# Third attention of a four-layer block: centred key and query weights, biases as matrix products, another order of the queues

## Chip, core and metric
One NeuronCore of a Trainium2 chip runs one program. The metric is the device time of one execution in microseconds; three executions were timed, and one more was profiled.

## What is computed
Four layers, each an attention-like part and a feed-forward network (FFN), add to one residual x of 1024 rows (4 batches of 256) by 256 columns. The change concerns the third attention:

```python
q = _ln((x @ Wq + bq).reshape(b, s1, H, HD), qn_w, qn_b)         # H = 16 heads, HD = 16
k_dca = _ln((y[:, -16:] @ Wkv_dca + bkv_dca)[keys], kn_dca_w, kn_dca_b)   # last 16 context rows
k = _ln(y[:, :-16] @ Wk + bk, kn_w, kn_b)                        # the other 240
ctx = softmax(q k / 4) v + softmax(q k_dca / 4) v_dca            # two softmaxes, added
x = x + ctx @ Wo + bo
```
The layer norm `_ln` works per head over 16 columns. (These lines are condensed.)

## The kernel before
Five in-order queues (TensorE, VectorE, ScalarE, GpSimd, SyncE for transfers) are written out by hand; counting semaphores tie them. Rows lie on 128 partitions in 8 tiles; `X` holds the residual. PSUM has 8 banks of 512 f32 columns. Work of neighbouring layers is interleaved by hand:
- **482.8 to 540** (times of the profile): the second FFN for its first 512 rows. TensorE's `gate_up(0, 0, c)` (L2338) makes chunk c of 8, ScalarE's `silu` and VectorE's `gate` (L1632) finish it. Between the chunks stand tiles 4 to 7 of the first, quantised FFN: `ffn0_gate_up`, `ffn0_gated` (L1428: two products, block maxima), GpSimd's scaling, `ffn0_round`, scaling, `hidden_transpose`, `ffn0_down`. `gate_up` chunk 6 asks for the first product of tile 7.
- **540 to 557**: the second attention's last batches, the norms, the four down products.
- **557 to 628.7**: the second FFN for the other 512 rows, 8 chunks and 4 down products, with the third attention's keys between. `K_STEPS` (L394) says which key steps stand after which chunk. A key batch is 256 context rows: `keys_values` (L2265) makes three products of 512 columns (keys and values of two tiles, and the 16 extra rows' own weights applied to the second tile). VectorE's `keys_step` (L1574) adds biases, masks, centres (`center`, L1507), squares and sums (`variance`), divides by the root (`over_deviation`), applies gains, and merges the third product's keys into the second tile. ScalarE takes the root (L954, with a table of its own, so that each use loads two tables).
- Keys and queries are split into three bf16 parts each, six slots of 16 columns a head (`kparts`): ScalarE's copies, and two subtractions on VectorE (L1614, L1595; L1744, L1746 for queries). TensorE transposes this stack in four quarters of four heads (`stack_transpose`, L2253), all through banks 0 and 1, and ScalarE copies each quarter out (`stack_out`, L981).
- `queries(hf, part)` (L1531) does the like for 512 query rows (four tiles, 1024 columns a pass): the first half between the down products, the second in batch 0's loop.
- **628.7 to 670.5**: query stacks of batches 0 and 1, then `scores` (L2479) for 16 heads of batch 0, each read by two maximum reductions (L1753 over 240 keys, L1754 over 16) from one of two banks, then `maxima_parts` (L1756).
- **670.5 to 820**: the loop over 4 batches of 16 heads. Each head has a transposed score with the maximum subtracted (`shifted`, L2497), `Exp`, and `values` (L2510). Beside them stand the next batch's scores and maxima, its query stack, the second queries (batch 0), `normalise` (L1766) every four heads, output products, and steps of a table lookup for the third FFN's weights (`lut_step`, L1785, with ScalarE's L1082). GpSimd makes `shiftw` (L661) before it.

## Time and profile before
| what | us |
|---|---|
| median of 3 runs (lowest, highest) | 1001.25 (999.36, 1004.71) |
| the profiled execution | 998.12 |
| its span | 996.30 |
| TensorE busy | 869.7 |
| VectorE busy | 681.3 |
| ScalarE busy | 547.3 |
| GpSimd busy | 360.5 |

The span runs from the first to the last instruction recorded; times in the views count from its start. Matrix products are pipelined, and their ends are modelled. An f32 product shows as two instructions. Engines are PE (TensorE), PEld (its weight loads), DVE (VectorE), ACT (ScalarE), POOL (GpSimd).

### The profile page before, as it was taken

To read this page: it belongs to the slowest core of one execution; us is meant where nothing else is said; L and a number is where in the kernel's file an instruction comes from. 1 tells how busy PE (TensorE), PEld (TensorE's weight loads), DVE (VectorE), ACT (ScalarE), POOL (GpSimd) and SP (SyncE) were. 2 spreads that over 40 slices of the span, in tenths; PEclk is the share of its full clock that TensorE was granted. 3 is DMA by queue.
4 is the path that set the end of the run, shared out by engine and by line. 5 is a ranking of instruction groups with operands and counts; after the bars stand their busy time and mean duration, and the time that the engine had idled before them with its cause. 6 is when DMAs were issued, how large, how long until landed. Compare 5 with 4: busy or idle time off the path is not lost.

```text
span 996.3 us, 13312 instructions
## 1 busy us (share of the span) xinstructions
PE 869.7 (87%) x4446; PEld 612.8 (62%) x4450; DVE 681.3 (68%) x1369; ACT 547.3 (55%) x1017; POOL 360.5 (36%) x249
## 2 busy tenths in 40 slices
PE   4797799999999999987888889458789899999998
PEld 3365587777778778744446546327578784554646
DVE  4347689899998988786765766666888872453211
ACT  2377577877877777974333444435678672012110
POOL 1211578787877778656443100030000000700000
PEclk9899899999999999999999999759699999999999
DMA  4003000001000000110302000000000002000000
GB/s 130 17 0 143 16 17 16 16 16 32 16 16 16 16 19 4 46 43 1 112 10 86 0 1 1 0 1 1 1 2 1 2 1 104 32 1 1 16 5 22
DMA packets 12926, 24.27 MB, mean 24 GB/s; under 512 B 4281, under 2 KB 8657, under 8 KB 11729
## 3 DMA queue, kind: packets, MB, share of 16 engines
q1 hardware_dynamic: 12448, 20.53, 6.5%
q10 hardware_dynamic: 432, 3.15, 0.8%
q8 instruction: 27, 0.44, 0.2%
q14 instruction: 19, 0.15, 0.0%
HBM read 22.63 MB, written 1.05 MB: 24 GB/s over the span
## 4 chain that ended last, share of the span: by engine, by line
PE 34%; DVE 15%; ACT 5%; issue 3%; POOL 2%; DMA 0%; ACTq 0%; DVEq 0%; POOLq 0%
PE PS L2344 14%; PE PS L2356 6%; PE PS L2522 3%; DVE mxf L1753 2%; PE PS L2131 1%; PE PS L2261 1%; PE PS L1865 1%; POOL regA L620 1%; ACT regC L1082 1%; PE PS L2204 1%; PE PS L2296 1%; PE PS L2486 1%; PE PS L2506 1%; PE PS L2507 1%; ACT regA L1097 1%
## 5 line engine op out<-in xcount | busy, mean ns | idle before, releaser
L541 POOL TENSOR_TENSOR X<-X,xn 128x512 f32<-128x512 f32 x62 | 103.4, 1668 | 69.0 <-ACT xn L771 68.3
L500 POOL TENSOR_SCALAR veps<-mv 128x4 f32<-128x4 f32 (+1 forms) x20 | 5.5, 275 | 299.9 <-DVE mv L1154 297.9
L1238 DVE TENSOR_SCALAR_CACHE_REDUCE regA<-PS,nrq 128x256 bf16<-128x256 f32 x128 | 56.0, 475 | 37.9 <-PE PS L1940 36.0
L1261 DVE TENSOR_TENSOR_SCAN regB<-regB 128x1024 f32<-128x1024 f32 x30 | 78.5, 2618 | 1.1 <-POOL regA L620 1.0
L534 POOL TENSOR_TENSOR y<-y,regB 128x1024 f32<-128x1024 f32 x32 | 75.6, 2365 | 9.4 <-DVE regB L1272 9.3
L795 ACT ACTIVATE regA<-PS,nb,rq 128x256 f32<-128x256 f32 x128 | 72.1, 576 | 11.7 <-DVE regA L1238 10.9
L2522 PE MATMUL PS<-regA 128*128 128x128 f32 x512 | 73.3, 289 | 3.4 <-ACT regA L1097 3.1
L1962 PE MATMUL PS<-regA 128*128 128x256 f32 x256 | 67.0, 384 | 7.3 <-DVE qss L1225 7.2
L2522 PEld LDWEIGHTS PS<-regA 128*128 128x128 f32 x512 | 66.5, 202 | 7.3 <-ACT regA L1097 6.2
L1940 PE MATMUL PS<-regA 128*128 128x256 f32 x256 | 67.8, 388 | 0.0
L1971 PE MATMUL PS<-regA 128*128 128x256 f32 x256 | 66.3, 382 | 0.0
L1913 PE MATMUL PS<-xnT,regA 128*128 128x512 f32 x128 | 60.6, 616 | 4.6 <-ACT regA L761 3.4
L2344 PE MATMUL PS<-xnT,regB 128*128 128x512 f32 x128 | 59.3, 609 | 1.4 <-DMA regB<-in_wd 1.4
L2356 PE MATMUL PS<-regB 128*128 128x256 f32 x256 | 57.0, 379 | 0.0
L2344 PE MATMUL PS<-regA,regB 128*128 128x512 f32 x128 | 55.8, 594 | 1.4 <-ACT regA L1010 1.4
L1962 PEld LDWEIGHTS PS<-regA 128*128 128x128 f32 x256 | 47.3, 192 | 14.2 <-DVE qss L1225 8.4
L1940 PEld LDWEIGHTS PS<-regA 128*128 128x128 f32 x256 | 46.4, 194 | 15.5 <-issue 10.1
L1002 ACT ACTIVATE regB<-PS 128x512 f32<-128x512 f32 (+1 forms) x28 | 16.7, 595 | 69.6 <-PE PS L2344 63.2
L801 ACT COPY regA<-PS 128x512 f32<-128x512 f32 x64 | 38.2, 596 | 29.8 <-PE PS L1951 29.6
L1640 DVE TENSOR_TENSOR regB<-regB,PS 128x512 f32<-128x512 f32 (+1 forms) x28 | 19.2, 686 | 50.9 <-ACT regB L1002 50.9
L1971 PEld LDWEIGHTS PS<-regA 128*128 128x128 f32 x256 | 49.2, 192 | 6.9
L771 ACT ACTIVATE xn<-PS,ls 128x256 f32<-128x256 f32 x124 | 52.8, 491 | 0.1
(285 smaller groups left out, 2103.8 us busy)
## 6 DMA issues: line engine op xcount, KB each, us to landing
regA<-in_W SPq DMA_DIRECT2D x16, 384.0 KB, 3.0
regB<-in_wg SPq DMA_DIRECT2D x2, 1024.0 KB, 6.3
regB<-in_wu SPq DMA_DIRECT2D x2, 1024.0 KB, 8.2
X<-in_x SPq DMA_DIRECT2D x1, 1024.0 KB, 8.1
regC<-in_wg ACTq DMA_DIRECT2D x1, 1024.0 KB, 5.9
regC<-in_wu ACTq DMA_DIRECT2D x1, 1024.0 KB, 8.0
regC<-in_wd ACTq DMA_DIRECT2D x1, 1024.0 KB, 11.1
regB<-in_wd SPq DMA_DIRECT2D x1, 1024.0 KB, 4.8
```

The source lines that it names most:

```text
L534: pool.tensor_tensor(halves(y3, i), halves(y3, i), halves(prod, i), ALU.add).then_inc(y_done, 1)
L541: pool.tensor_tensor(xt, xt, part, ALU.add).then_inc(x0_add, 1)
L795: act.activation(p0[i][:, q, :], bank(S_BANK + i)[:, q * S:(q + 1) * S], ACT.Exp, bias=nb0[:, i, q:q + 1], scale=rq[par][:, 2 * b + q:2 * ...
L1238: ins = dve.tensor_scalar(spill[:, i, q, :], bank(S_BANK + i)[:, q * S:(q + 1) * S], nrq[par][:, t:t + 1], None, ALU.mult, ALU.min, accum_ ...
L1261: dve.tensor_tensor_scan(v(hs), v(decays), v(dBu), 0.0, ALU.mult, ALU.add).then_inc(scan_done, 1)
L1913: last = pe.matmul(to[:, i * HALF:(i + 1) * HALF], w0[par][:, c * P:(c + 1) * P], xnT[:, c, i * HALF:(i + 1) * HALF], start=c == 0, stop=c ...
L1940: last = pe.matmul(bank(S_BANK + b % 2)[:, q * S:(q + 1) * S], qT[par][:, (2 * b + q) * P:(2 * b + q + 1) * P], kT[par][:, b * S:(b + 1) * S],
L1962: last = pe.matmul(bank(O_BANK)[:, 0:S], ctxN[:, 2 * b + k, :], pT0[b % 2][:, k, :], start=k == 0, stop=k == 1)
L1971: last = pe.matmul(bank(W_BANK)[:, q * DIM:(q + 1) * DIM], oT0[b % 2][:, q * P:(q + 1) * P], wvo[par], start=True, stop=True)
L2344: last = pe.matmul(bank(to)[0:rows, :], w[:, k, c * P:c * P + rows], src[:, k, :], start=k == 0, stop=k == KD - 1)
L2356: last = pe.matmul(bank(6 + td % 2)[:, 0:DIM], hT[0:rows, c, t * P:(t + 1) * P], wd[0:rows, c, :], start=c == 0, stop=c == nch - 1)
L2522: last = pe.matmul(bank(6 + g % 2)[:, at:at + P], pT2[i % 3][:, k, q * P:(q + 1) * P], V2flat[:, v:v + P], start=k == 0, stop=k == 1)
```

## The change
1. VectorE subtracts each head's mean over its 16 columns from the key and query weights and biases (`center_weights`, four steps between pieces of the first FFN), so that projections come out centred. The biases become three bf16 parts, and TensorE adds them by a product with a 0/1 matrix, `pick`.
2. A key batch takes two tiles in place of three. GpSimd copies the 16 extra context rows into `ctx_extra` (zeros elsewhere) and zeroes them in `ctxT`, so that their product adds into the second tile's bank. Gains come laid out per row (`gain_k`).
3. ScalarE squares out of PSUM and copies and masks the values; VectorE sums squares, divides out of PSUM and applies gains. ScalarE's root takes scale and offset.
4. Stack quarters 1 and 3 are copied out by VectorE (until the first query stack), 0 and 2 by ScalarE.
5. The first queries move among the chunks (after chunk 3), and the order of all queues around them is rewritten. The scores of batch 0 use four banks and stand between the down products.
6. A maximum is one reduction into groups of 16 keys, joined once a batch. `normalise` does one product in place of two; GpSimd adds the output bias. Steps in the loop move by a head (`STACK2`, `LNT9`, `QPROJ`, `QNORM`). Some buffers share memory in another way.

The core of the diff (eight leading blanks dropped):

```diff
+bc3 = max_groups[0:96].rearrange("p h q g -> p (h q g)").bitcast(BF16)
...
+KV_BANK = [4, 6, 6, 6]
+NORM2 = ["k0", "k1", "k2", "q0", "k3", "q1"]
...
+def by_vector(k):
+    return k < 4 * (B + 1) and k % 2
+def copied(k):
+    if by_vector(k):
+        return stk_copy, sum(1 for i in range(k + 1) if by_vector(i))
+    return stk_out, sum(1 for i in range(k + 1) if not by_vector(i))
+def score_bank(b, h):
+    return 2 + (h % 4 if b == 0 else h % 2)
...
+    for tile, name in ((wkv2, "wkv2"), (wdca2, "wdca2"), (wq2, "wq2"), (bias_rows, "b2"), (pick_rows, "pick"), (wo2, "wo2")):
         sp.dma_start(tile, a[name]).then_inc(ld_2, 16)
-    for tile, name, n in ((bkv2[:, 0:DIM], "bk2", DIM), (bkv2[:, DIM:], "bv2", DIM), (bdca2, "bdca2", 2 * DIM),
-                          (bq2, "bq2", DIM), (bo2, "bo2", DIM)):
-        sp.dma_start(tile, a[name].to_broadcast([P, n])).then_inc(ld_2, 16)
...
+    last_keys = ctxT[:, :].rearrange("p (b two k) -> p b two k", b=B, two=2)[:, :, 1, MAIN - P:]
+    pool.wait_ge(y_done, 2 * NST + 1)
+    pool.wait_ge(qk1_mm, 2)
+    pool.memset(ctx_extra[:, :, 0:MAIN - P], 0.0).then_inc(ctx_set, 1)
+    pool.tensor_copy(ctx_extra[:, :, MAIN - P:], last_keys).then_inc(ctx_set, 1)
+    pool.wait_ge(ctx_set, 2)
...
+    def output_bias(hf):
+        pool.wait_ge(*xn_ready(8 + hf))
+        for i in range(2):
+            xt = X[:, TPH * hf + 2 * i:TPH * hf + 2 * i + 2, :]
+            pool.tensor_tensor(xt, xt, bo2.unsqueeze(1).to_broadcast([P, 2, DIM]), ALU.add).then_inc(bo2_add, 1)
...
+    def squares(name):
+        dst = qs[int(name[1])] if name[0] == "q" else k_sq
+        if name[0] == "q":
+            act.wait_ge(q2_mm, int(name[1]) + 1)
+        else:
+            act.wait_ge(kv2_mm, int(name[1]) + 1)
+        if name in ("k1", "k2", "k3"):
+            act.wait_ge(var2, norm2("k%d" % (int(name[1]) - 1)))
+        act.activation(dst.rearrange("p t h d -> p t (h d)") if name[0] == "k" else dst.rearrange("p (a t) h d -> p a (t h d)", a=2),
+                       qk_bank(name).rearrange("p a h d -> p a (h d)"), ACT.Square).then_inc(sq2, 1)
+    def values_out(b):
+        act.wait_ge(kv2_mm, b + 1)
+        v = [bank(KV_BANK[b] + t)[:, DIM:].rearrange("p (h d) -> p h d", h=H2) for t in range(2)]
+        act.copy(V2[:, 2 * b, :, 0:HD2], v[0])
+        act.activation(V2[:, 2 * b + 1, :, 0:HD2], v[1], ACT.Copy, scale=mask[:, 0:1])
+        act.activation(V2[:, 2 * b + 1, :, HD2 + 1:VW - 1], v[1], ACT.Copy, scale=mask[:, 1:2]).then_inc(v2_out, 1)
+    def deviations(name):
+        lo, n = (4, TPH) if name[0] == "q" else (0, 2)
+        act.wait_ge(var2, norm2(name))
+        act.activation(r2[:, lo:lo + n, :], m2[:, lo:lo + n, :], ACT.Sqrt, scale=1.0 / HD2, bias=qk_eps[:, 0:1]).then_inc(dev2, 1)
...
+    silu(0, 1, 0)
+    squares("k1")
+    values_out(1)
+    silu(0, 1, 1)
+    stack_even(0)
+    ln_apply(8)
+    deviations("k1")
+    silu(0, 1, 2)
     ln_out(8)
...
+    keys_high(1)
+    keys_mid(1)
+    silu(0, 1, 3)
+    squares("k2")
+    squares("q0")
+    values_out(2)
+    silu(0, 1, 4)
+    deviations("k2")
+    deviations("q0")
+    stack_even(1)
+    silu(0, 1, 5)
+    keys_high(2)
+    squares("k3")
+    keys_mid(2)
+    values_out(3)
+    silu(0, 1, 6)
+    deviations("k3")
+    stack_even(2)
+    keys_high(3)
+    silu(0, 1, 7)
+    keys_mid(3)
+    stack_high(0)
+    stack_even(3)
+    stack_mid(0)
+    stack_even(B)
...
+    def center_weights(step):
+        dve.wait_ge(ld_2, LD2)
+        if step == 0:
+            both = regC[:, 0:4 * DIM].rearrange("p (w s h d) -> p w s h d", w=2, s=2, h=H2)[:, :, 0]
+            center(both, m2[:, 8:10, :]).then_inc(w2_ready, 1)
+        elif step == 1:
+            center(groups(wq2.rearrange("p k n -> p (k n)")), m2[:, 10:12, :].rearrange("p a h -> p (a h)")).then_inc(w2_ready, 1)
+        elif step == 2:
+            dve.tensor_copy(pick.rearrange("p a m -> p (a m)"), pick_rows).then_inc(w2_ready, 1)
+            link(center(groups(bias_rows[:, 0:2 * DIM]), m2[0:96, 6:8, :].rearrange("p a h -> p (a h)")))
+        else:
+            link(dve.tensor_copy(bias3, bias_rows))
+            link(dve.tensor_tensor(bias_rows, bias_rows, bias3, ALU.subtract))
+            dve.tensor_copy(bias3[32:64], bias_rows[32:64])
+            link(dve.tensor_copy(bias3[64:96], bias_rows[64:96]))
+            link(dve.tensor_tensor(bias_rows[64:96], bias_rows[64:96], bias3[64:96], ALU.subtract))
+            dve.tensor_copy(bias3[64:96], bias_rows[64:96]).then_inc(w2_ready, 1)
+    def variances(name):
+        lo, n, v = (4, TPH, qs[int(name[1])]) if name[0] == "q" else (0, 2, k_sq)
+        dve.wait_ge(sq2, norm2(name))
+        dve.tensor_reduce(m2[:, lo:lo + n, :], v, AX.X, ALU.add).then_inc(var2, 1)
+    def normed(name):
+        b = int(name[1])
+        lo, n, v = (4, TPH, qf[b % 2]) if name[0] == "q" else (0, 2, kf)
+        r, flat_r = r2[:, lo:lo + n, :], r2[:, lo:lo + n, :].rearrange("p t h -> p (t h)")
+        dve.wait_ge(dev2, norm2(name))
+        link(dve.reciprocal(r, r))
+        if name[0] == "q":
+            src = qk_bank(name)
+            by = flat_r.rearrange("p (a g) -> p a g", a=2).unsqueeze(3).to_broadcast([P, 2, 2 * H2, HD2])
+            link(dve.tensor_tensor(v.rearrange("p (a t) h d -> p a (t h) d", a=2), src, by, ALU.mult))
+            dve.sem_inc(q2_out, 1)
+            wide = [P, TPH * H2, HD2]
+            link(dve.tensor_tensor(rows_of(v), rows_of(v), ln2[:, 0, :].unsqueeze(1).to_broadcast(wide), ALU.mult))
+            dve.tensor_tensor(rows_of(v), rows_of(v), ln2[:, 1, :].unsqueeze(1).to_broadcast(wide), ALU.add).then_inc(stk_f, 1)
+        else:
+            wide = [P, 2, H2, HD2]
+            link(dve.tensor_tensor(v, qk_bank(name), r.unsqueeze(3).to_broadcast(wide), ALU.mult))
+            dve.sem_inc(kv2_use, 1)
+            link(dve.tensor_tensor(v, v, gain_k[:, 0].unsqueeze(2).to_broadcast(wide), ALU.mult))
+            dve.tensor_tensor(v, v, gain_k[:, 1].unsqueeze(2).to_broadcast(wide), ALU.add).then_inc(stk_f, 1)
+    def keys_rest(b):
+        dve.wait_ge(stk_h, b + 1)
+        dve.tensor_tensor(ks2, kf2, kparts[:, :, 0, :], ALU.subtract).then_inc(stk_r, 1)
+    def keys_low(b):
+        dve.wait_ge(stk_m, b + 1)
+        dve.tensor_tensor(kparts[:, :, 2, :], ks2, kparts[:, :, 1, :], ALU.subtract).then_inc(stk_done, 1)
+    def stack_odd(j):
+        for c in (1, 3):
+            b = j % B
+            dve.wait_ge(stk_tr, 4 * j + c + 1)
+            src = bank(1).bitcast(BF16)[0:STK, :].rearrange("p (h t) -> p h t", h=HPB)
+            heads = slice(HPB * c, HPB * c + HPB)
+            dve.tensor_copy(ksT[:, heads, b * S:(b + 1) * S] if j < B else qsT[b % 2][:, heads, :], src).then_inc(stk_copy, 1)
...
     gate(0, 0, 2)
     ffn0_round(4)
     gate(0, 0, 3)
+    center_weights(0)
     ffn0_gated(5)
     gate(0, 0, 4)
     ffn0_round(5)
+    center_weights(1)
     ffn0_add(4)
     ffn0_gated(6)
     gate(0, 0, 5)
     ffn0_round(6)
+    center_weights(2)
     ffn0_add(5)
+    center_weights(3)
     ffn0_gated(7)
...
+    gate(0, 1, 0)
+    variances("k1")
+    stack_odd(0)
+    gate(0, 1, 1)
+    normed("k1")
+    keys_rest(1)
+    gate(0, 1, 2)
+    keys_low(1)
+    gate(0, 1, 3)
+    variances("k2")
+    variances("q0")
+    gate(0, 1, 4)
+    normed("k2")
+    normed("q0")
+    stack_odd(1)
+    keys_rest(2)
+    gate(0, 1, 5)
+    variances("k3")
+    keys_low(2)
+    gate(0, 1, 6)
+    normed("k3")
+    stack_odd(2)
+    keys_rest(3)
+    gate(0, 1, 7)
+    keys_low(3)
     ffn_add(0, 1, 0)
...
+    stack_rest(0)
+    stack_odd(3)
+    stack_low(0)
+    stack_odd(B)
...
-        sc = bank(2 + h % 2).rearrange("p (q k) -> p q k", q=2)
         dve.wait_ge(s2_mm, i + 1)
-        dve.tensor_reduce(mxf[:, :, h, 0], sc[:, :, 0:MAIN], AX.X, ALU.max)
-        dve.tensor_reduce(mxf[:, :, h, 1], sc[:, :, MAIN:], AX.X, ALU.max).then_inc(max2, 1)
+        dve.tensor_reduce(max_groups[:, h], bank(score_bank(b, h)).rearrange("p (q g k) -> p q g k", q=2, k=DCA), AX.X,
+                          ALU.max).then_inc(max2, 1)
...
+        dve.tensor_reduce(mxf[:, :, :, 0].rearrange("p q h -> p h q"), max_groups[:, :, :, 0:MAIN // DCA], AX.X, ALU.max)
+        link(dve.tensor_copy(mxf[:, :, :, 1].rearrange("p q h -> p h q"), max_groups[:, :, :, MAIN // DCA]))
...
+        link(dve.reciprocal(rl2[:, :, :].rearrange("p n s -> p (n s)"), o[:, :, HD2]))
+        link(dve.tensor_tensor(co2.rearrange("p n s d -> p (n s) d"), o[:, :, 0:HD2],
+                               rl2[:, :, :].rearrange("p n s -> p (n s)").unsqueeze(2).to_broadcast([P, 4 * HPB, HD2]), ALU.mult))
+        parts = co2.rearrange("p (h q) s d -> p q h s d", q=2)
+        dve.tensor_tensor(co[:, :, HPB * g:HPB * g + HPB, :], parts[:, :, :, 0, :], parts[:, :, :, 1, :], ALU.add).then_inc(o2_norm, 1)
...
+        if b == 0:
+            pe.wait_ge(w2_ready, 4)
+            pe.wait_ge(ctx_set, 3)
+            pe.wait_ge(gated, FC)
+        elif b == 1:
+            pe.wait_ge(df_add, TPH)
         else:
...
+            pe.wait_ge(kv2_use, b)
+            pe.wait_ge(v2_out, b)
+        for t in range(2):
+            to, td = bank(KV_BANK[b] + t), 2 * b + t
+            pe.matmul(to, ctxT[:, td * P:(td + 1) * P], wkv2, start=True, stop=False)
+            if t:
+                pe.matmul(to, ctx_extra[:, b, :], wdca2, start=False, stop=False)
+            last = pe.matmul(to, pick[:, t, :], bias3[:, DIM:], start=False, stop=True)
+        last.then_inc(kv2_mm, 1)
...
+                    pe.matmul(to, xnT[:, k, td * P:(td + 1) * P], wq2[:, k, :], start=k == 0, stop=False)
+                last = pe.matmul(to, pick[:, 0, :], bias3[:, 0:DIM], start=False, stop=True)
+        last.then_inc(q2_mm, 1)
...
-    ln_transpose(8)
+        if c == 0:
+            keys_values(1)
+        elif c == 1:
+            stack_keys(0)
+        elif c == 2:
+            pe.wait_ge(*copied(2))
+            pe.wait_ge(*copied(3))
+            ln_transpose(8)
+        elif c == 3:
+            keys_values(2)
+            queries(0)
+        elif c == 4:
+            pe.wait_ge(q2_out, 1)
+            stack_keys(1)
+        elif c == 5:
+            keys_values(3)
+        elif c == 6:
+            stack_keys(2)
+    pe.wait_ge(kv2_use, B)
+    pe.wait_ge(v2_out, B)
     pe.wait_ge(df_add, TPH)
...
+        pe.wait_ge(*copied(4 * (B + b) + h // HPB))
+        if b == 0 and h < 4:
+            pe.wait_ge(gated, 2 * FC)
+        elif b == 0:
+            pe.wait_ge(max2, h - 3)
+        elif h >= 2:
             pe.wait_ge(max2, i - 1)
+        else:
+            pe.wait_ge(max2, b * H2)
         for q in range(2):
-            last = pe.matmul(bank(2 + h % 2)[:, q * S:(q + 1) * S], qsT[b % 2][:, h, q * P:(q + 1) * P],
+            last = pe.matmul(bank(score_bank(b, h))[:, q * S:(q + 1) * S], qsT[b % 2][:, h, q * P:(q + 1) * P],
...
+        if h % HPB == HPB - 1 and h < H2 - 1:
+            pe.wait_ge(df_add, TPH + h // HPB)
+            down(0, 1, h // HPB + 1, wf_d)
```

## Rows read from the trace of the kernel before
**Rows 1.** The page, parts 1 and 2: busy time, and granted clock by slice.
```profile
PE 869.7 (87%) x4446; PEld 612.8 (62%) x4450; DVE 681.3 (68%) x1369; ACT 547.3 (55%) x1017; POOL 360.5 (36%) x249
...
PEclk9899899999999999999999999759699999999999
```

**Rows 2.** Windows: stretch in us; its length; busy us (instructions) per engine; clock; DMA share, GB/s.
```profile
482.82:540.00 57.18, 48.49 (x196) 23.66 (x196) 35.70 (x60) 18.83 (x30) 24.97 (x21) 1.00 0.26 78
...
557.00:608.50 51.50, 42.74 (x148) 21.17 (x147) 39.57 (x89) 28.50 (x36) 1.86 (x4) 0.93 0.00 0
608.50:628.70 20.20, 20.16 (x120) 17.71 (x120) 13.70 (x23) 6.44 (x8) 0.00 (x0) 1.00 0.00 1
628.70:670.50 41.80, 16.64 (x99) 9.18 (x99) 25.11 (x57) 15.86 (x18) 7.02 (x1) 0.61 0.00 1
670.50:718.00 47.50, 37.08 (x255) 32.04 (x255) 34.96 (x82) 26.42 (x36) 1.27 (x2) 0.77 0.00 1
718.00:753.00 35.00, 28.41 (x249) 24.89 (x249) 29.34 (x73) 27.58 (x42) 0.00 (x0) 1.00 0.00 1
```

**Rows 3.** Timeline, TensorE: start us, us, engine, line, operation, count, [idle before <- releaser].
```profile
624.20 1.06 PE L2261 MATMUL PS<-identb,regB 128*96 128x128 bf16 x16
...
637.95 1.94 PE L2261 MATMUL PS<-identb,regB 128*96 128x128 bf16 x16 [9.18 <-DVE regB L1595]
...
647.24 1.91 PE L2261 MATMUL PS<-identb,regB 128*96 128x128 bf16 x16 [5.42 <-DVE regB L1746]
...
657.21 1.25 PE L2486 MATMUL PS<-regA,regB 96*128 96x256 bf16 x4 [5.22 <-DVE mxf L1754]
```

**Rows 4.** Groups by shape, 557 to 670.5, VectorE: busy us, mean ns | idle before.
```profile
L1753 DVE TENSOR_REDUCE mxf<-PS 128x2 f32<-128x480 f32 x16 | 10.5, 656 | 0.7
...
L1520 DVE TENSOR_TENSOR regB<-regB,r 128x768 f32<-128x768 f32 x4 | 3.8, 958 | 0.1
...
L1754 DVE TENSOR_REDUCE mxf<-PS 128x2 f32<-128x32 f32 x16 | 2.9, 182 | 0.0
...
L1606 DVE TENSOR_TENSOR regB<-regB,ln 128x512 f32<-128x512 f32 x4 | 2.8, 692 | 0.1
...
L1519 DVE RECIPROCAL r<-r 128x48 f32<-128x48 f32 x3 | 1.4, 453 | 1.7 <-ACT r L954 1.7
L1550 DVE TENSOR_TENSOR regB<-regB,ln 128x1024 f32<-128x1024 f32 x1 | 1.2, 1226 | 0.0
```

**Rows 5.** The same view, 0 to 480, VectorE: its casts to bf16.
```profile
L1186 DVE CAST bc<-PS 96x512 bf16<-96x512 f32 x2 | 1.4, 686 | 2.1 <-PE PS L1880 2.0
...
L1188 DVE CAST bc<-regC 32x512 bf16<-32x512 f32 x2 | 0.8, 416 | 0.1
```

**Rows 6.** Timeline, VectorE and TensorE, around 523.
```profile
522.13 1.48 DVE L1435 TENSOR_TENSOR regA<-regA,PS 128x512 f32<-128x512 f32 x2 [0.18 <-ACT regA L910]
...
524.25 3.65 PE L2344 MATMUL PS<-xnT,regB 128*128 128x512 f32 x8
```

**Rows 7.** Groups by shape, 557 to 670.5, ScalarE.
```profile
L987 ACT COPY regA<-PS 96x1024 bf16<-96x1024 bf16 x16 | 15.3, 1007 | 20.9 <-PE PS L2261 20.9
L1002 ACT ACTIVATE regB<-PS 128x512 f32<-128x512 f32 x8 | 4.8, 594 | 6.2 <-PE PS L2344 6.2
...
L1072 ACT COPY regB<-PS 96x256 bf16<-96x256 bf16 x1 | 0.4, 368 | 14.3 <-PE PS L2493 14.3
```

**Rows 8.** Timeline, TensorE: two chunks of gate and up products.
```profile
571.63 4.34 PE L2344 MATMUL PS<-xnT,regB 128*128 128x512 f32 x8
...
576.70 3.65 PE L2344 MATMUL PS<-xnT,regB 128*128 128x512 f32 x8
```

**Rows 9.** Timeline, ScalarE: a table load and the instruction behind it.
```profile
562.26 1.28 ACT L1002 ACT_TABLE_LOAD   x1
563.55 0.60 ACT L1002 ACTIVATE regB<-PS 128x512 f32<-128x512 f32 x1
```

**Rows 10.** Timeline, TensorE: a wait for maxima in batch 0's loop.
```profile
696.59 0.58 PE L2486 MATMUL PS<-regA,regB 96*128 96x256 bf16 x2 [3.64 <-DVE mxf L1754]
```

417 lines of the change are left out of this document (166 added, 251 removed).

## The prediction
> **What bounds the kernel now.** I read the page first: TensorE is busy 87% of the span at a clock granted 8 tenths or more nearly everywhere, except in two slices, 7 and 5 [rows 1]. A stretch where TensorE idles and is slow is where a rescheduling can pay. The table of stretches places it [rows 2]. Six stretches matter: 482.8 to 540 (the first half of the second FFN interleaved with the quantised one), 557 to 608.5 (second half, gate and up products, with the key batches between), 608.5 to 628.7 (down products, first queries), 628.7 to 670.5 (query stacks, scores, maxima of batch 0), 670.5 to 718 (loop over the heads of batch 0), and a later batch. In the fourth TensorE works 16.6 of 41.8 us at a clock of 0.61; batch 0's loop takes 47.5 us where the next takes 35. From 557 to 670.5 VectorE is busy 39.6 + 13.7 + 25.1 = 78.4 of 113.5 us. The timeline shows TensorE waiting for VectorE's norms and splits: gaps of 9.2, 5.4 and 5.2 us [rows 3]. The same work hangs from one queue in batch 0's loop, where VectorE is busy 35.0 us.
>
> **The centring of weights, 482.8 to 540.** New: VectorE centres the key and query weights and builds three-part bf16 biases in four steps, between pieces of the FFN. Steps 0 and 1 are a reduce, a small scale and a subtract over 512 columns: 0.7 + 0.2 + 0.7 = 1.6 us each, by the 512-column row [rows 4]. Step 2 is a small cast and the same on 96 partitions, 1.8. Step 3 is four casts of 768 columns (0.55 each, from 0.42 for 512 [rows 5]) and two subtracts of 0.96 [rows 4], 4.1. Sum 9.1 us. VectorE idles 57.2 - 35.7 = 21.5 us here [rows 2], but the places are bad. Step 0 stands right behind a gate and ahead of the quantised FFN's tile 5, step 1 ahead of tile 6; each hands on most of its 1.6 us. Steps 2 and 3 (5.9 us) stand ahead of its last tile, now at 522.13 after a wait of 0.18 [rows 6]. TensorE's chunk 6 waits for the first half of that tile and starts at 524.25, some 1.4 us after it. Tile 7 comes 1.7 (the delay handed on from steps 0 and 1) + 5.9 late, chunk 6 is 7.6 - 1.4 = 6.2 late, and the last hidden block, behind it, as much. I take **+7 us**, with 0.3 for the three bias products, plus 1 for the gap's clock: **+8**. Bounds: 1 (all falls into idle time) and 11 (the 9.1 whole, and 2 of clock). The new waits ahead of the first key product (weights, context, gate 7) end with or before that tile; behind them stand attention 1 and the down products, all shifted by the same 8. SP issues 11 transfers in place of 13 on that semaphore, before its wait for the quantised FFN's last product, as now; the index loads behind move with the 8 and have 100 us. GpSimd's zeroing and copying of context columns, some 1 us, falls into idle time.
>
> **One key batch.** VectorE now spends eight instructions on copying, biasing and masking out of PSUM, five 768-column passes (0.96 each), six on gains and masks, two of 0.69 on splits: 13 us. After: a reduce of 512, a reciprocal of some 0.4, three passes of 512 (0.69 [rows 4]), two splits, 4.6 us, plus two of the four stack copies that ScalarE has at 1.0 us each [rows 7]. No row copies bf16 from PSUM on VectorE. The nearest is 96x512 of f32 at 0.69 [rows 5], so for 1024 columns twice that less the overlap; bounds 0.8 (twice the SBUF cast's 0.42) and 1.37. I take 1.15, the nearest: 6.9 us in all. The Trainium skill ("VectorE: DVE Perf Modes", the perf-mode tier table) lets a copy that touches PSUM reach up to 2x when all is 16-bit; by it a copy would take 0.6 and the stretch would end 1.4 us earlier. ScalarE gains a square (0.6) and three value copies (0.4 each) [rows 7].
>
> **The queries.** Ten passes (two of 512, eight of 1024 columns) with smalls, 10.8 us per half, become a reduce, a reciprocal of 0.55 and three passes of 1.23 [rows 4]: 5.5 us.
>
> **The stretch 557 to 670.5, as one schedule.** I laid the four queues out in order with these durations, 0.15 us from a signal to its waiter, and TensorE at the upper clock: 3.5 us a chunk [rows 8], 3.0 for a key product (6 x 0.43, two bf16 bias products of 0.22), 3.9 for the queries, 0.45 per stack quarter (16 transposes take 1.06 with overlap [rows 3]), 0.22 per head of scores. TensorE's sum is 68. The stops:
> 1. Each set of four transposes waits for copies: 0.8 us, five times.
> 2. After chunk 4 comes a wait of 6.7 us: it asks for the first queries' read-out from PSUM, which on VectorE stands behind key batch 2, which waits for ScalarE's square roots, which stand behind silu of that very chunk. Then 1.4 more for the copy behind the query gains.
> 3. Chunk 6's stack waits 2.4 + 2.3 for the roots and copies of batch 3, the query stack 2.3 for its low part.
> 4. The last four heads' maxima and the five small steps behind (1.75) leave 4.0 and 0.7 idle before the first shifted score.
> These make 23.9, and the first shifted score comes 92 us after the start, against 113.5: **-21.5**. Gate and up alone end at 61.5, later than 51.5 now, since the queries are among them; scores and maxima hide between down products, which cover 12 of the 16. A chunk behind a wait took 4.34 us at a lower clock, for 3.65 [rows 8]; two such losses after stop 2: **+1.5**. Bounds for the stretch: -30 (stop 2 gone) and -12 (the clock low for half of it).
> The root tables: 1.28 us a load; eight here, as the schedule has them. In the trace the silu starts 0.01 us after its load's end [rows 9]. The Trainium skill ("ScalarE: Activation LUTs", what ACT_TABLE_LOAD costs) adds a drain of 1.38 us to each; the row speaks against it, and by it my schedule would end 2.8 us later.
>
> **The loop, 670.5 to 820.** Batch 0: TensorE waits for VectorE, up to 3.64 us, while the second queries' passes stand ahead of the maxima [rows 10], so 10.8 - 5.5 = 5.3 us of query work come off; with one block of queries in place of three, some 2 more of low clock (0.77 [rows 2]): -7. A maximum is one pass of 512, at 0.62, for 0.66 + 0.18 overlapped to 0.67 [rows 4]; the joining of groups costs 0.85 a batch: 16 x 0.05 - 0.85, nothing. Normalisation and the output bias, moved to idle GpSimd (4 additions), take 0.3 us off each batch. Together **-8**; bounds 0 and -12. Behind 820 nothing changes.
>
> **Sum:** +8 - 21.5 + 1.5 - 8 = -20. The profiled execution took 998.12 (span 996.30), 3.1 under the median of 1001.25; I set the difference against the median: **981 us**.
>
> **The rivals.**
> *The centring is covered and the loop runs freer.* For it: 21.5 idle us of VectorE, so a delay can be absorbed. Then +2 instead of +8 and -11 instead of -8: 972. Against: the two late steps come in one block before a tile that two chunks ask for.
> *In-order queues tie up.* Three engines now hand each key batch around inside one chunk; any estimate 0.3 us short is paid at each hand-over, about 30 of them: +9, 990. For it: stops 2 and 3 are of this kind already. Against: each link above is priced from a row.
> *Slower: TensorE stays at 1.2 GHz from stop 2 on.* The place is the 6.7 us gap after chunk 4. The schedule behind it holds 36 us of TensorE work and 15 of waiting: at the lower clock +36 - 15 = +21. Batch 0's loop has 37.1 x 0.77 = 28.6 us of work, 57 at the lower level against my 40: +17. Together 981 + 38 = 1019. It decides from the point where the clock is still low when the loop begins: by then 21 us have gone, of 20 gained, and every further head costs. For it: 0.61 over 41.8 us now, with gaps of this size. Against: a chunk at a lower clock took 4.34 us and the next 3.65 [rows 8], so chunks bring the clock back, and three follow. The Trainium skill ("TensorE: Matmul & The Clock Gate", HAM oscillation) warns of just such gaps between bursts; the rows agree that the clock falls, and that it returns.
> *No gain:* stretch at its bound -12, centring at 11, loop 0: 1000.
>
> **How the numbers follow.** A difference of 0.5% is about what a measurement of this kernel can tell from none. Forecast 0.60 (its own range 973 to 989), freer 0.15, tied up 0.16, no gain 0.05, slow clock 0.04. No gain and slow clock (0.09) lie outside the range, and a third of the two rivals beside the forecast (0.10): 966 to 994. Faster by over 0.5%: 0.60 + 0.15 + 0.16 = 0.91, and 0.01 of the fourth; same 0.04, slower 0.04.
>
> **What would show it.** (a) TensorE idle for some 5 us ahead of chunk 6 of the first half, ended by VectorE. (b) From that half's last down product to the first shifted score about 92 us. (c) A TensorE gap of 5 to 8 us after the fifth chunk, ended by VectorE. (d) Batch 0's loop about 40 us, the next 34 to 35. (e) VectorE's stack copies at 1.15. (f) Clock over 0.85 in the stretch now at 0.61. It is wrong if (b) exceeds 105, if chunk 6 does not wait, or if the loop keeps its 47 us.

## The result, and the profile after
The kernel after takes **991.98 us** (median of 6, 989.88 to 994.31), the kernel before, beside it, 1001.24 (median of 6): a ratio of 0.9906 with a 95% interval of 0.9882 to 0.9929. It is faster, by 9.3 us, where 20 were forecast: 0.9%, and the interval leaves out 1. The profiled execution took 989.88 us, with a span of 988.1. So the two profiles differ by 8.2 us of span. The page of the kernel after answers to [rows 1]:

```profile
PE 871.6 (88%) x4462; PEld 615.1 (62%) x4466; DVE 653.4 (66%) x1237; ACT 546.9 (55%) x1026; POOL 366.3 (37%) x257
...
PEclk8899799999999999999997998889899999899999
```
VectorE has 28 us less work, and the slices at 7 and 5 of [rows 1] are gone, and the one at 6 two slices later. But the clock now dips (the 7 in slice 22, 519 to 543 us) where the second FFN's first half stands. Five marks split the span in both profiles: the first chunk of the second FFN's first half, that of its second half, the first shifted score, the transposes of batch 1's maxima, and the third FFN's first chunk (stretches 1 to 5 start there).

| stretch | before | after | difference | forecast |
|---|---|---|---|---|
| ahead of 1 | 487.7 | 488.3 | +0.7 | 0 |
| 1: first half, with the quantised tiles | 69.6 | 81.3 | +11.7 | +8 |
| 2: second half, to the first shifted score | 113.3 | 96.0 | -17.2 | -20 |
| 3: batch 0's loop, to batch 1's maxima | 47.4 | 42.8 | -4.6 | -7 |
| 4: the other batches | 104.5 | 102.8 | -1.7 | -1 |
| 5: third FFN and all behind | 173.9 | 176.8 | +2.9 | 0 |

The windows of the kernel after, as in [rows 2] (the last two lines are stretches 1 and 2 as a whole):

```profile
483.00:540.00 57.00, 42.90 (x149) 19.33 (x150) 40.48 (x60) 14.45 (x22) 21.70 (x16) 0.88 0.15 48
570.00:622.00 52.00, 44.10 (x183) 24.04 (x182) 25.20 (x48) 29.04 (x45) 4.35 (x6) 0.93 0.00 0
622.00:634.50 12.50, 8.58 (x38) 5.15 (x36) 5.28 (x9) 7.37 (x10) 0.00 (x0) 0.73 0.01 1
634.50:665.70 31.20, 22.88 (x160) 19.08 (x158) 21.54 (x38) 9.05 (x10) 7.02 (x1) 0.90 0.00 1
665.70:708.50 42.80, 34.17 (x257) 29.34 (x258) 30.75 (x63) 28.47 (x39) 4.11 (x4) 0.88 0.00 1
720.00:754.00 34.00, 28.90 (x253) 25.52 (x252) 29.48 (x60) 26.19 (x41) 0.00 (x0) 1.00 0.00 1
488.33:569.66 81.33, 68.24 (x270) 39.72 (x273) 47.66 (x86) 25.91 (x42) 27.44 (x32) 0.92 0.14 47
569.66:665.70 96.04, 75.91 (x376) 48.46 (x374) 52.02 (x94) 45.80 (x63) 11.37 (x7) 0.90 0.00 1
```
Before, stretch 1 ran at a granted clock of 1.00, now at 0.92. The loss there is gaps and clock together. The timeline of TensorE in stretch 1, after:

```profile
508.98 3.70 PE L2488 MATMUL PS<-xnT,regB 128*128 128x512 f32 x8 [0.65 <-DVE regA L1551]
...
519.03 5.40 PE L2488 MATMUL PS<-xnT,regB 128*128 128x512 f32 x8 [1.59 <-DVE regA L1551]
...
534.59 6.25 PE L2488 MATMUL PS<-xnT,regB 128*128 128x512 f32 x8 [5.40 <-DVE regA L1551]
```
Three chunks wait for the quantised tiles, 7.6 us in all. Two of them then take 5.40 and 6.25 us in place of 3.65 [rows 8], 4.3 us more at the lower clock. VectorE's and GpSimd's timelines show one step ahead of those waits:

```profile
514.55 0.68 DVE L1626 TENSOR_REDUCE m<-regC 128x32 f32<-128x512 f32 x1
515.26 1.46 DVE L1627 TENSOR_SCALAR m<-m 128x32 f32<-128x32 f32 x1
516.76 0.69 DVE L1628 TENSOR_TENSOR regC<-regC,m 128x512 f32<-128x512 f32 x1
```
```profile
514.78 1.91 POOL L662 TENSOR_TENSOR regA<-regA,mx_s 128x1024 bf16<-128x1024 fp8e4 x1 [1.20 <-DVE regA L1523]
```
The scale of 32 columns, 0.18 us elsewhere, ends when GpSimd's instruction does (514.78 + 1.91 = 516.69). In step 2 it takes 1.26 in the same way, so 2.4 us of VectorE's queue are such holds (below, "held" means this: an instruction on VectorE that lasts until GpSimd's ends). The Trainium skill ("SBUF — State Buffer", section "Who interferes with whom") describes this: VectorE and GpSimd share a pair of ports, and a fast copy or scale, or an instruction with two SBUF inputs, blocks until the other engine's instruction is through (in the last case only if GpSimd's reads SBUF). The trace agrees: the two scales end with GpSimd's instruction.

In stretch 2 the stops stand where they were forecast ("stack 2" below is the set of transposes of key batch 2, and so on):

```profile
607.38 1.94 PE L2405 MATMUL PS<-identb,regB 128*96 128x128 bf16 x16 [6.78 <-DVEq L1666]
...
624.88 0.88 PE L2405 MATMUL PS<-identb,regB 128*96 128x128 bf16 x8 [2.41 <-ACT regA L1057]
...
627.26 1.06 PE L2405 MATMUL PS<-identb,regB 128*96 128x128 bf16 x8 [1.50 <-DVE regA L1694]
...
642.13 1.94 PE L2405 MATMUL PS<-identb,regB 128*96 128x128 bf16 x16 [2.32 <-DVE regB L1854]
...
664.73 0.42 PE L2646 MATMUL PS<-identb,mxs 128*96 128x128 bf16 x2 [3.89 <-DVE mxs L1904]
```
Sixteen transposes behind a stop take 1.94 us, elsewhere 1.06. TensorE is idle for 20.1 us of the 96.0 in all (34.0 of 113.3 before). One hold was not foreseen: the lookup table's subtract, beside GpSimd's product for `shiftw` (VectorE, then GpSimd):

```profile
646.66 2.60 DVE L1921 TENSOR_TENSOR lutd<-lut 128x8 f32<-128x8 f32 x1
```
```profile
642.22 7.02 POOL L719 TENSOR_TENSOR regC<-regC 96x4096 bf16<-96x4096 f32 x1 [54.56 <-DVE regB L1854]
```

### The profile page after: what moved, and what is told of

Its sections match the earlier page's. It is cut to its first block, busy times and chain, and to the rows that moved or that the text cites. A ratio compares the mean times of both kernels' runs of the same rounds, so it can differ in the third digit from the quotient of the medians.

```text
span 988.1 us, 13238 instructions
## 1 busy us (share of the span) xinstructions
PE 871.6 (88%) x4462; PEld 615.1 (62%) x4466; DVE 653.4 (66%) x1237; ACT 546.9 (55%) x1026; POOL 366.3 (37%) x257
## 4 chain that ended last, share of the span: by engine, by line
PE 39%; DVE 11%; ACT 4%; issue 3%; POOL 1%; DMA 0%; ACTq 0%; DVEq 0%
PE PS L2488 16%; PE PS L2500 7%; PE PS L2675 3%; DVE max_groups L1891 2%; PE PS L2405 1%; PE PS L2275 1%; PE PS L2009 1%; PE PS L2348 1%; PE PS L2659 1%; PE PS L2440 1%; PE PS L2422 1%; PE PS L2660 1%; ACT regB L1077 1%; ACT regC L1197 1%; DVE regB L1937 1%
## 5 line engine op out<-in xcount | busy, mean ns | idle before, releaser
L583 POOL TENSOR_TENSOR X<-X,xn 128x512 f32<-128x512 f32 x62 | 103.5, 1669 | 68.8 <-ACT xn L829 68.0
L853 ACT ACTIVATE regA<-PS,nb,rq 128x256 f32<-128x256 f32 x128 | 72.0, 575 | 11.7 <-DVE regA L1354 10.9
L2675 PE MATMUL PS<-regA 128*128 128x128 f32 x512 | 71.3, 284 | 4.0 <-ACT regA L1210 3.9
L2488 PE MATMUL PS<-xnT,regB 128*128 128x512 f32 x128 | 64.3, 650 | 8.9 <-DVE regA L1551 7.6
L2500 PEld LDWEIGHTS PS<-regB 128*128 128x128 f32 x256 | 48.1, 190 | 7.6 <-issue 1.4
```

Source lines behind the costliest of these rows:

```text
L583: pool.tensor_tensor(xt, xt, part, ALU.add).then_inc(x0_add, 1)
L853: act.activation(p0[i][:, q, :], bank(S_BANK + i)[:, q * S:(q + 1) * S], ACT.Exp, bias=nb0[:, i, q:q + 1], scale=rq[par][:, 2 * b + q:2 * ...
L2488: last = pe.matmul(bank(to)[0:rows, :], w[:, k, c * P:c * P + rows], src[:, k, :], start=k == 0, stop=k == KD - 1)
L2500: last = pe.matmul(bank(6 + td % 2)[:, 0:DIM], hT[0:rows, c, t * P:(t + 1) * P], wd[0:rows, c, :], start=c == 0, stop=c == nch - 1)
L2675: last = pe.matmul(bank(6 + g % 2)[:, at:at + P], pT2[i % 3][:, k, q * P:(q + 1) * P], V2flat[:, v:v + P], start=k == 0, stop=k == 1)
```

## The experiments
Each kernel is the kernel after with one edit, unless said otherwise; "stretch 1" and so on come from its one profile. How far does a stretch repeat where nothing in it was edited? With the kernel after counted in, stretch 1 took 81.3 to 81.6 us (9 profiles) and stretch 2 took 95.6 to 97.5 (7; 96.0 to 96.2 in the 3 whose stretch 1 was unedited too). Stretch 3 took 42.6 to 44.5 (13), stretch 4 102.8 to 106.2 and stretch 5 173.5 to 176.8 (all 15). Effects under these spreads can't be read from one profile, and the intervals of most single edits' totals overlap with that of the kernel after (0.9882 to 0.9929).

| kernel | median us | ratio to before, 95% | 1 | 2 | 3 | 4 | 5 |
|---|---|---|---|---|---|---|---|
| before_again | 1000.63 | 1.0012 (0.9993 to 1.0032) | 69.6 | 113.6 | 47.5 | 104.5 | 175.4 |
| no_centre | 983.03 | 0.9819 (0.9787 to 0.9852) | 71.3 | 95.9 | 44.5 | 105.0 | 175.2 |
| c_moved | 989.80 | 0.9893 (0.9859 to 0.9927) | 78.4 | 95.6 | 44.4 | 105.0 | 175.2 |
| c_moved_stt | 986.61 | 0.9849 (0.9808 to 0.9891) | 73.0 | 97.5 | 43.0 | 103.5 | 175.2 |
| centre_spread | 982.26 | 0.9815 (0.9775 to 0.9855) | 69.9 | 96.7 | 42.9 | 102.9 | 176.8 |
| q0_first | 988.82 | 0.9885 (0.9852 to 0.9919) | 81.4 | 95.4 | 43.1 | 103.5 | 175.2 |
| roots_early | 987.71 | 0.9883 (0.9866 to 0.9899) | 81.3 | 92.2 | 42.9 | 103.5 | 175.2 |
| stacks_first | 990.27 | 0.9908 (0.9879 to 0.9937) | 81.4 | 94.0 | 43.8 | 104.1 | 175.1 |
| copies_scalar | 989.68 | 0.9902 (0.9883 to 0.9922) | 81.5 | 94.5 | 43.6 | 106.2 | 173.6 |
| scores_after | 992.69 | 0.9928 (0.9902 to 0.9954) | 81.3 | 99.6 | 42.6 | 102.9 | 175.2 |
| lutd_early | 990.68 | 0.9899 (0.9858 to 0.9940) | 81.4 | 95.1 | 43.2 | 106.2 | 173.6 |
| split_q1 | 993.66 | 0.9922 (0.9896 to 0.9948) | 81.6 | 96.2 | 43.8 | 105.5 | 175.2 |
| no_q1_gains | 990.28 | 0.9904 (0.9871 to 0.9937) | 81.4 | 96.1 | 40.5 | 105.4 | 175.2 |
| joined | 976.73 | 0.9755 (0.9729 to 0.9781) | 69.9 | 88.3 | 43.7 | 106.2 | 173.5 |
| joined_scalar | 975.33 | 0.9748 (0.9720 to 0.9775) | 71.6 | 93.3 | 44.0 | 104.2 | 175.2 |

**What the centring costs (no_centre).**
```diff
 if step == 2:
     dve.tensor_copy(pick..., pick_rows).then_inc(w2_ready, 1)
-    link(center(groups(bias_rows[:, 0:2 * DIM]), ...))
-else: (casts and subtracts of three parts)
+elif step == 3:
+    dve.tensor_copy(bias3, bias_rows).then_inc(w2_ready, 3)
```


> Leaves out the centring of the key and query weights and of the biases, and the second and third bf16 parts of the biases: VectorE keeps one small cast and one cast of 768 columns of about 9 us of steps. Theory (the missing gain is the centring, whose places delay chunks 4 to 6 of the quantised second FFN half and cost clock behind each gap): the stretch from the first chunk of the second FFN's first half to the first chunk of its second half, 69.6 us before and 81.3 us after the change, comes to 71 +- 1.5, TensorE no longer waits over 1 us ahead of chunks 5 and 6, nothing else moves by over 2 us, and the total is 982 +- 2. Rival (the hand-over of the third attention's first key batch or the longer FFN order makes it, and the centring only fills idle time): the stretch stays over 78 and the total over 988.

Left out are the centring and two of the three parts of the biases. Stretch 1 fell to 71.3, the total by 9 us. The theory stands: some 10 of the 11.7 us are the centring's own. The one large cast left was held as well: it took 2.02 us for 0.55, and chunk 6 waited 0.31 us and took 5.40.

**The same steps elsewhere (c_moved, and c_moved_stt).**
```diff
 ffn0_round(4)
-gate(0, 0, 3)
 center_weights(0)
+gate(0, 0, 3)
 ffn0_gated(5)
+center_weights(1)
...
 ffn0_gated(7)
 layer_norm_stats(6, 0)
+center_weights(3)
...
 ffn0_add(6)
+center_weights(4)
```


> The whole change, with the same centring steps at other places of VectorE's order: step 0 ahead of gate 3 in place of behind it, steps 1 and 2 behind the quantised FFN's tiles 5 and 6 in place of ahead of tiles 6 and 7, step 3 cut in two, both halves behind tile 7. Theory (the price is the place: what stands ahead of a tile delays a chunk): the stretch of 81.3 us comes to 74 +- 2, chunk 6's wait of 5.4 us to under 1.5, total 985 +- 2. Rival (VectorE lacks the time, wherever the 9 us stand): the waits only move to chunks 7 and the first down product, the stretch stays over 79, total 990 or more.

78.4: neither as forecast nor unchanged. The wait ahead of chunk 6 went. The waits inside the quantised tiles stayed or grew: 1.73, 2.11, 0.77 and 1.71 us, where the kernel after has 0.55, 0.84, 0.77 and 1.56. One chunk took 5.17 us. So the place alone isn't the price. The small scale took 1.46, 1.45 and 1.26, and the large casts 1.60 and 2.10: with GpSimd busy twice 1.91 us in each tile's 8 to 11, other places of VectorE's order meet it too.
```diff
-link(dve.tensor_scalar(mean, mean, 1.0 / HD2, None, ALU.mult))
-return dve.tensor_tensor(v, v, mean..., ALU.subtract)
+return dve.scalar_tensor_tensor(v, mean..., -1.0 / HD2, v, ALU.mult, ALU.add)
```


> As c_moved, with the small scale (TENSOR_SCALAR of 32 columns, which took 1.46, 1.45 and 1.26 us beside a GpSimd instruction, for 0.18 alone) and the 512-column subtract joined into one scalar_tensor_tensor with both inputs in SBUF. Theory by the Trainium skill's SBUF page (an instruction with two SBUF inputs also waits for a GpSimd instruction that reads SBUF): the joined instruction is held instead, 1.5 to 2.1 us for 0.69, and only 0.2 to 0.3 us a step are saved; the stretch of 78.4 us in c_moved comes to 77.5 +- 1. Rival (only the small fast-mode instruction is held): 0.69 us each, VectorE gains 4 us, the stretch comes to 75 or less.

Of the instruction the Trainium skill ("SBUF — State Buffer", section "Who interferes with whom") is right. VectorE's timeline in c_moved_stt:
```profile
508.40 0.68 DVE L1626 TENSOR_REDUCE m<-regC 128x32 f32<-128x512 f32 x1
509.11 1.97 DVE L1627 SCALAR_TENSOR_TENSOR regC<-m,regC 128x512 f32<-128x512 f32 x1
```
The reduce beside it, with one input, is not held. Of the time both expectations fell: the stretch came to 73.0. From the pair of chunks 2 and 3 to tile 6's transposes, c_moved took 29.28 us and this kernel 28.63, the 0.65 that three joined steps save. The other 4.7 us are clock: 0.93 in c_moved's stretch, 1.00 in this one. Behind the same gap of 1.71 us c_moved's next chunk took 5.17 us and this kernel's 3.65. What decides the clock there stays open. The medians are 3.2 us apart, and no execution of one kernel reaches the other's (988.1 to 990.8, 984.4 to 987.0), so it isn't the chance of one profile alone; with a forecast of 74 +- 2, c_moved missed.

**Centring on three engines (centre_spread).**
```diff
 VectorE:  +group_sums(step): the three tensor_reduce alone; last subtract and cast
 GpSimd, behind hidden(4), hidden(5):
+    pool.tensor_scalar(mean, mean, 1.0 / HD2, None, ALU.mult)
+    pool.tensor_tensor(v, v, mean..., ALU.subtract)
 GpSimd, behind hidden(6):  +pool.tensor_tensor(bias_rows, bias_rows, bias3, ALU.subtract)
 ScalarE, behind hidden_out(5), hidden_out(6):  +act.copy(bias3..., bias_rows...) three times
```


> The whole change, with the centring given to three engines: VectorE keeps the three group sums (0.68 us each), one small cast, the last 768-column subtract and cast; GpSimd takes the scale and the subtracts, behind its conversion of tiles 4, 5 and 6 (it idles 2.6 to 5 us there); ScalarE takes three bias casts. Theory (9 us of VectorE work do not fit beside the quantised FFN, whose tile needs VectorE, GpSimd and TensorE in turn, so that every us ahead of a tile is paid, and only other engines' idle time is free): the stretch of 81.3 us comes to 73.5 +- 1.5, total 984 +- 2. Rival (the port that VectorE's and GpSimd's instructions contend for makes GpSimd's extra instructions as costly as VectorE's were): VectorE's small instructions take over 1 us in several places, the stretch stays over 77.

Better than expected: 69.9, as in the kernel before, at a clock of 1.00. GpSimd's timeline shows what it takes there:
```profile
506.40 1.91 POOL L671 TENSOR_TENSOR regA<-regA,mx_s 128x1024 bf16<-128x1024 fp8e4 x1 [0.87 <-DVE regA L1547]
508.40 0.31 POOL L710 TENSOR_SCALAR m<-m 128x32 f32<-128x32 f32 x1
508.79 1.06 POOL L712 TENSOR_TENSOR regC<-regC,m 128x512 f32<-128x512 f32 x1
```
The scales and subtracts stand in GpSimd's own queue, so nothing of GpSimd's runs beside them, and its idle time between tiles covers them. No chunk waits for a tile any more. One hold is left, VectorE's last subtract, and it costs nothing, since no tile stands behind it:
```profile
532.59 2.50 DVE L1657 TENSOR_TENSOR regC<-regC 32x768 f32<-32x768 f32 x1
```
Place, engine and hold change at once here, so the run doesn't part their shares.

**Stop 2: whose queue? (q0_first, roots_early).**
```diff
 gate(0, 1, 4)
-normed("k2")
-normed("q0")
-stack_odd(1)
+normed("q0", then=lambda: (stack_odd(1), normed("k2")))   # then: behind the read-out
```


> The whole change, but VectorE reads the first queries out of PSUM, and copies their waiting key stack, ahead of key batch 2's norms instead of behind them. Theory (the gap of 6.8 us after the fifth chunk is the in-order queue): key batch 2's block of about 2.9 us goes from the wait, the gap is 3.9 +- 0.5, and the first shifted score comes 2 to 3 us earlier; total 989.5 +- 2. Rival (the work is only exchanged): the gap shrinks by as much, but the wait ahead of chunk 6's stack, 2.4 us now, grows by 2 to 3 us, and the total stays at 992.

The gap fell from 6.78 to 4.47 us, but two chunks behind took 4.85 and 6.16 us (3.65 and 5.54 before the edit), and the stretch came to 95.4, 0.1 under the lowest unedited one. The rival is right in the sum of the stretch, but by the clock more than by batch 2's parts: the second gap in stack 2 grew by 0.26 us only. (The median, 988.82, is as the theory had it, but its interval overlaps with that of the kernel after.)
```diff
 squares("q0")
 values_out(2)
-silu(0, 1, 4)
 deviations("k2")
 deviations("q0")
+silu(0, 1, 4)
```
(and VectorE's gate 4 behind the read-out)

> The whole change, with ScalarE's square roots of key batch 2 and of the first queries ahead of the silu of the fifth chunk, and VectorE's read-out of these queries ahead of that chunk's gate, the stack copies and key batch 2's norms. In the kernel with only VectorE's order changed the gap after the fifth chunk fell from 6.8 to 4.5 us and two chunks behind gave most of it back at a lower clock. Theory (the roots wait for that silu in ScalarE's queue; the two table loads are the same in number): the read-out ends at about 603.4 in place of 607.3 us, the gap is 2.8 +- 0.6, and since it is short the chunk behind takes 3.65 to 4.3 us; the stretch of 96.0 us comes to 92 +- 1.2, total 988 +- 2. Rival (the stretch is held by key batches 2 and 3 behind: their parts come as late as before): the waits ahead of chunk 7's stack and query stack grow, the stretch stays over 94.5.

As the theory said. TensorE's timeline in roots_early:
```profile
604.38 1.09 PE L2404 MATMUL PS<-identb,regB 128*96 128x128 bf16 x16 [2.47 <-DVEq L1666]
606.22 1.91 PE L2404 MATMUL PS<-identb,regB 128*96 128x128 bf16 x16 [0.74 <-ACT regA L1057]
607.92 4.33 PE L2487 MATMUL PS<-xnT,regB 128*128 128x512 f32 x8
```
At 2.47 us of gap the first sixteen transposes run at the upper clock (1.09), the next at the lower, and the stretch is 3.8 us shorter.

**The copies in stack 2 (stacks_first) and part 4 undone (copies_scalar).**
```diff
-deviations("k3")
 stack_even(2)
+deviations("k3")
...
-normed("k3")
 stack_odd(2)
+normed("k3")
```
(and `stack_odd(1)` ahead of the query gains)

> The whole change, with the copies of key stacks 1 and 2 ahead of the gains of the first queries and ahead of the roots and norms of key batch 3, which stand before them in VectorE's and ScalarE's queues. Theory (the gaps of 2.4 and 1.5 us in stack 2 and of 0.3 in stack 1 are copies queued behind these): the two gaps fall to under 0.7 each, batch 3's parts come 1.5 us later and take 1 us of it back in the wait of the last stack; the stretch of 96.0 us comes to 94 +- 1. Rival (exchanged in full): 95.5 to 97, with the gap ahead of the query stack grown from 2.3 to over 4 us.

94.0, as the theory said: the gaps of 2.41 and 1.50 us in stack 2 came down to 0.78, chunk 7 took 3.65 us for 5.54, and a wait of 2.44 us for the last gate came in the first down product.
```diff
-return k < 4 * (B + 1) and k % 2
+return False                          # by_vector: all copies by ScalarE
```


> Undoes one part: all copies of transposed stacks on ScalarE again (1.01 us each), none on VectorE (0.69). Theory (two banks in turn, each freed by its copy: with one engine the four copies of a set take 4 x 1.01 in line, with two engines the pairs overlap): each of the five sets takes 1.1 to 1.5 us longer, the stretch of 96.0 us comes to 101 +- 2, total +4 to +6. Rival (ScalarE has the time, and VectorE is relieved of 10 x 0.69 us): 96 to 97.5, total within 2.

The theory fell: 94.5, 1.5 us shorter, and under the rival's 96 too. A set costs only 0.3 us more, and the 1.50 us gap behind VectorE's copy, which queues behind key batch 3's norms, is gone; chunk 7 took 4.52 us for 5.54, which is clock. Part 4 of the change was worth nothing here.

**Scores between the down products (scores_after).**
```diff
+for t in range(1, TPH): (wait, down(0, 1, t, wf_d))
 for h in range(H2):
     scores(0, h)
-    if h % HPB == HPB - 1 and h < H2 - 1: (wait, down(0, 1, h // HPB + 1, wf_d))
```
(VectorE's order likewise)

> Undoes one part: batch 0's scores and maxima stand behind the last down product again, not between the down products. Theory (maxima on VectorE, 16 x 0.67 = 10.7 us, were hidden between down products, of which the first twelve heads count): the first shifted score comes 7 to 9 us later, total +8 +- 2, 1000. Rival (VectorE's queue is the bound there either way, since the down products' sums and the low parts stand in it): +3 or less. Second rival (the clock falls in the stretch of short matmuls and stays low in batch 0's loop): +12 or more.

+3.6 us in the stretch, between theory and rival; the theory was twice too high. The total's +0.7 is within its noise. An account that fits, worked out afterwards and not tested by itself: twelve heads' maxima hidden are 7.4 us. But with the scores between, their own products (0.9 us a group of four) stand in line with the down products, 2.7 us, where otherwise they run beside the maxima. And the table subtract, held in both kernels (2.60 and 2.61 us), counts only with the scores between, 0.9 us by the next run. 7.4 - 2.7 - 0.9 is 3.8.

**The table subtract (lutd_early).**
```diff
 ones_of_odd_tiles()
+dve.tensor_tensor(lutd[:, :], lp[:, :, 1], lp[:, :, 0], ALU.subtract)
```


> The whole change, with one 128x8 subtract of the lookup table (0.16 us in the kernel before, 2.60 us here, ending with GpSimd's 96x4096 product) moved from ahead of batch 0's maxima to the begin of the second half. Theory (VectorE's instruction is held until GpSimd's ends, and the maxima stand behind it): it takes 0.2 us at the new place, the scores behind the query stack come 2.4 us earlier, and the stretch of 96.0 us comes to 93.6 +- 0.6; total -2. Rival (the maxima's chain is ended by something else, the down products and their sums): the stretch moves by under 1 us.

The rival, narrowly: 0.9 us (95.1, for 96.0 to 96.2 in the three profiles with stretches 1 and 2 unedited). The subtract is short at its new place (0.16 us) and the maxima come 2.5 us earlier, but each later group's sum then waits 1.3 to 1.5 us for its down product.

**Batch 0's loop (split_q1, no_q1_gains).**
```diff
 if b == 0 and h == QNORM + 2:
     normed("q1")                      # without gain and bias
+if b == 0 and h == QNORM + 3:
+    query_gains(1)
```


> The whole change, with the second queries' gain and bias passes (2 x 1.23 us) one head later in batch 0's loop than their read-out from PSUM, so that the maxima of a head stand between. Theory (TensorE's 4.0 us gap at 700.6 us waits for maxima behind that block): the gap falls to 1.6 +- 0.6, and the lower clock behind it (8 us at 1.2 GHz) goes in part; batch 0's loop, 42.8 us, comes to 39.5 +- 1.5. Rival (the wait is only handed to the next head, whose maxima now stand behind the second half of the block): 42 to 43.

43.8: nearer the rival, but by another way. TensorE's timeline in the kernel after (first line) and in split_q1 (the others):
```profile
700.60 1.18 PE L2639 MATMUL PS<-regA,regB 96*128 96x256 bf16 x4 [4.02 <-DVE max_groups L1891]
```
```profile
702.53 1.18 PE L2648 MATMUL PS<-regA,regB 96*128 96x256 bf16 x4 [1.62 <-DVE max_groups L1898]
...
709.23 2.07 PE L2684 MATMUL PS<-regA 128*128 128x128 f32 x8 [2.95 <-ACT regA L1210]
```
The gap for the maxima fell from 4.02 to 1.62 us, and a new one of 2.95 came a head later. ScalarE's exponential ends it, not the maxima, and it stands in ScalarE's queue behind the casts of the second queries, which wait for VectorE's gains (a cast that had waited 5.66 us for them):
```profile
705.41 1.47 ACT L1133 CAST regB<-regB 128x1536 bf16<-128x1536 f32 x1 [5.66 <-DVE regB L1659]
```

```diff
-(q1's two tensor_tensor passes with ln2)
+dve.sem_inc(stk_f, 1)
```


> The whole change, but the second queries get no gain and bias (two VectorE passes of 1.23 us are left out in batch 0's loop). Theory (TensorE's 4.0 us gap there is the VectorE queue as a whole: 4.3 us of query passes, 1.5 of lookup picks, 0.95 of normalisation): the gap falls by 2.4 to 1.6 +- 0.4 us, and batch 0's loop from 42.8 (42.6 to 44.5 in the variants) to 40 +- 1, the rest of it being the lower clock. Rival (the exponentials or the clock set the loop's length): 42 or more.

TensorE's timeline in that kernel has the gap at 1.73, and stretch 3 took 40.5 us, 2.3 less than in the kernel after and 2.1 less than in any of the 13 profiles with that stretch unedited. So the passes (2.46 us) are on the path at about their full price.
```profile
698.22 0.38 PE L2642 MATMUL PS<-regA,regB 96*128 96x256 bf16 x2 [1.73 <-DVE max_groups L1894]
```

**The tail (before_again).**

> The kernel before, unchanged, for a second profile of it: how far do its stretches vary by the clock alone? By the profiles so far, the kernel after and its variants took 173.6, 175.2 or 176.8 us from the third FFN's first chunk to the end, by whether the matmuls behind one gap of 1.96 us ran at 1.2 or 2.4 GHz, and 102.8 to 106.2 us for the later batches. Theory (chance of the clock, no effect of the change behind 811 us): this profile has 173.6 to 176.8 in the tail too, or the first profile's 173.9, and 113 +- 1 and 69.6 +- 0.6 in the two stretches that the change touches. Rival (the change itself costs 1.3 us in the tail): 173.9 +- 0.3 again.

Stretches 1 to 4 repeat within 0.3 us. The part ahead of them, which the table leaves out, does not: 492.4 us for 487.7 (487.1 to 492.3 over the kernel after and its variants, with no edit there). The tail took 175.4 in place of 173.9. The same products behind the same gap, in the kernel after (first line) and in lutd_early (second):
```profile
842.34 4.64 PE L2500 MATMUL PS<-regD,regB 128*128 128x256 f32 x12 [1.96 <-DVE X L1759]
```
```profile
845.21 3.05 PE L2500 MATMUL PS<-regD,regB 128*128 128x256 f32 x12 [1.96 <-DVE X L1759]
```
The kernel before has 3.05 us there in one profile and 4.55 in the other. And the 15 profiles with the tail of the kernel after lie at 173.5 to 176.8, on both sides of 173.9. So no cost of the change shows in the tail: 1.5 of the +2.9 lies within what the kernel before does itself, and the rest within what the kernel after does.

**Joined.** The edits of centre_spread, roots_early, lutd_early, and stack 2's order.

> The whole change with four corrections joined: the centring on three engines, the roots of key batch 2 and the first queries ahead of the fifth chunk's silu, stack 2's copies ahead of key batch 3's roots and norms, and the lookup subtract at the begin of the second half. Theory (the terms lie in different places and add): the first stretch 70 +- 1 and the second 96 - 3.8 - 1.5 = 90.5 +- 1.5, total 991.9 - 11.4 - 5.3 = 975 +- 2.5. Rival (what is gained in gaps comes back as lower clock and in later waits, as with the copies and the query read-out): second stretch over 93, total 979 or more.

```diff
-return k < 4 * (B + 1) and k % 2
+return False                          # joined_scalar
```


> As joined, with all copies of transposed stacks on ScalarE. With the change as it is this made the second stretch 1.5 us shorter, where 5 us longer was expected. Theory (VectorE's queue is the bound of that stretch, ScalarE's is not, and 10 x 0.69 us on VectorE cost more than 0.3 us a copy on ScalarE): 0.5 to 2 us faster than joined. Rival (the shorter stretch came only from stack 2's copies no longer standing behind key batch 3's norms on VectorE, which joined has mended): 0 to 3 us slower than joined.

They add, and the rival (979 or more) falls. 976.73, where 975 +- 2.5 was expected, is some 15 us under the kernel after, and 0.9755 (0.9729 to 0.9781) of the kernel before. Stretch 2 came to 88.3, under the forecast. Its profiled execution (973.15) was the fastest of its five, though, with the clock at 0.965. For joined_scalar the profile caught its slowest. Behind the same gap of 2.47 us the next chunk took 3.65 us in joined and 5.65 here, and stretch 1, which the two share, took 69.9 and 71.6. The medians, 1.4 us apart, don't settle who copies best.

## Why the prediction was right or wrong
The mechanisms were right in kind: (a), (c) and (d) showed, at 5.40 us ahead of chunk 6, a gap of 6.78 after the fifth chunk, and 42.8 us in batch 0's loop with 34.3 in the next ones (102.8 over three); (b) came at 96 for 92, and (f) with 0.90 from 634.5 us on, 0.73 in the 12.5 us ahead. What failed is sizes, all toward too little gain: of 11.8 us of span, 3.7 lie in stretch 1, 2.8 in stretch 2, 1.7 in the loop, 2.9 in the tail, 0.7 ahead. The common step that failed is what a gap costs in clock: priced at 1 us in stretch 1 and 1.5 in stretch 2, it came to 4.3 and some 8 (75.9 us of TensorE's time, for a schedule of 68).
- **Centring, "+8": 11.7.** The forecast's 7 us answer to 7.6 us of waits. They were laid ahead of chunk 6 alone; chunks 4 and 5 wait too (0.65 and 1.59 us), and chunk 5 is one of the two slow ones. The term "plus 1 for the gap's clock" was mis-sized most: 4.3 us. no_centre puts the whole of the centring, waits and clock included, at 10.0. VectorE's own sum of 9.1 lacked 2.4 us of holds by GpSimd; no row of before had such a pair, and I priced the small scale at 0.2. How much of the 2.4 lay on the path was not measured. centre_spread shows that the same arithmetic can cost nothing, given to other engines at other places; c_moved shows that the place alone gives 2.9.
- **Stretch 2, "-21.5 + 1.5": -17.2.** Four stops were right to 0.1 us each (6.78 for 6.7, 2.41 for 2.4, 2.32 for 2.3, 3.89 for 4.0). The copies' were too long: 1.50 for 2.3 in stack 2, 0.34 for 1.4 behind the query gains. In all TensorE idled 20.1 us where the stops were put at 23.9 (their terms add to 23.8). The mis-sized term is TensorE's own time, 68 + 1.5 for 75.9 us: the clock was sized at two chunks, while chunk 7 (5.54 us) and four sets of transposes (1.61 to 1.97 for 1.06) ran slow. The two errors cancel in part, which is luck. The held subtract (2.60 us, of which 0.9 counts) was not in the sum.
- **(e)** VectorE's stack copies took 0.69 us, not 1.15. The 0.6 estimated from the Trainium skill ("VectorE: DVE Perf Modes", perf-mode tier table) was nearer than my row of f32; the sum gained nothing by it, since copying on VectorE brought nothing (copies_scalar).
- **Loop, "-8": -6.3.** Batch 0 gave 4.6 of 7. (Here too the clock was low before: [rows 1] has a third low slice, at 6, from 697 to 722 us, which the prediction's reading of it passes over.) The 5.3 us of query work did go from VectorE, but TensorE's idle time fell only from 10.4 to 8.6 us; the other 2.8 are clock (0.77 to 0.88), for 2 forecast. So the failed step is that 5.3 us off VectorE's queue are 5.3 us off the loop. The remaining passes stand as one block with lookup picks and a normalisation behind, and TensorE waits 4.02 us there, where it waited 3.64 [rows 10]. no_q1_gains shows them on the path; split_q1 shows that ScalarE's queue, with casts that wait for them, holds the loop as well. And -6.3 is near the best of the range: over the 13 profiles with an unedited stretch 3, stretches 3 and 4 together gained 2.0 to 6.4 us on the kernel before, 4.2 in the mean.
- **"Behind 820 nothing changes": +2.9** in these profiles. No run shows a cost of the change there; half of it the kernel before shows between its own two profiles.
- **The rival "in-order queues tie up", 990**, had the number nearly, but not the reason: the hand-overs in stretch 2 cost less than forecast (20.1 for 23.9 us), not more.
- **Median against profile.** Each profile comes from an execution quicker than the kernel's median (by 3.1 and 2.1 us), so the medians differ by 1.0 us more than the two profiles.

## What to carry to other kernels
Idle time of an engine in a window says little of whether work fits: ask whether the next item on the path passes through that engine behind it, and which other engine is idle at the very place; giving the subtracts and casts to GpSimd and ScalarE made 11 us of cost vanish. A gap on TensorE costs itself and then, in these traces, from nothing to about as much again in slow chunks, so price both, and compare stretches over several profiles. Beside an instruction of GpSimd a 32-column scale on VectorE took 1.26 to 1.46 us for 0.18, so look what GpSimd runs at that moment.

## What the hardware showed that was not expected
- A 128x8 subtract on VectorE took 2.60 us and a 32-column scale 1.46, each ending with GpSimd's instruction; a reduce with one input beside it ran at its usual 0.68.
- Behind the same 1.96 us gap twelve products took 3.05 or 4.64 us, in executions of one and the same kernel too (3.05 and 4.55 in the two profiles of the kernel before).
- Shortening a gap from 6.78 to 4.47 us (q0_first) gave next to nothing, to 2.47 us (roots_early) gave 3.8: the transposes behind took 1.94, 1.94 and 1.09. But the same 2.47 us were followed by a chunk of 4.33 us in roots_early, 3.65 in joined and 5.65 in joined_scalar.
